# Router logits by linearity: the router's columns ride in the context products of the MLP

## The chip, the cores and the metric

The kernel runs on one core of one Trainium2 chip. The metric is the device time of one execution in microseconds, the median of three runs; lower is better. The engines have queues of their own and meet only at semaphores: TensorE (PE, with its weight loads PEld), VectorE (DVE), ScalarE (ACT), GpSimd (POOL) and SyncE (SP), which issues most of the transfers.

## The reference

`x` is 2 x 1024 tokens of 256 values. Four layers follow one another, each added to `x`: cross attention, attention with four chosen heads, an MLP whose weights are the context itself, and a mixture of eight experts with one expert per token. The change touches the last two.

```python
# third layer: w1 = w2 = ctx_1024[b], 77 x 256
def _L1_xattn_ref(x, w1, w2):              # x here is layernorm(x)
    h = jnp.einsum('eth,efh->etf', x, w1)  # 77 hidden values per token
    g = jax.nn.gelu(h, approximate=True)
    out = jnp.einsum('etf,efh->eth', g, w2)

# fourth layer, x here is layernorm of the new x
    logits = jnp.einsum('bsh,he->bse', x, w_router)
    probs = jax.nn.softmax(logits, axis=-1)
    sel = jnp.argmax(probs, axis=-1)
    wgt = probs at sel
    for e in range(n_experts):
        h = jax.nn.relu(xt @ w1[e] + b1[e])
        y = h @ w2[e] + b2[e]
        out = out + ((sel_t == e) * wgt_t)[:, None] * y
```

## The kernel before

The program is a row of blocks, one after the other: every engine must reach the end of a block before any enters the next. Here the blocks `context_mlp` (it ends at line 1208) and `experts` matter. Everything ahead of them, 390 us, is left as it is.

`context_mlp` works on the 2048 tokens in 16 tiles of 128, in four chunks n = 0 to 3 of four tiles. The order on each engine is written out by hand.

- PE first finishes the attention before it: `attended(r)`, r = 0 to 7, two tiles each. DVE adds the result to `x_all` (`attended` of DVE), takes mean and variance (`statistics`, BN_STATS and BN_AGGR), POOL takes the root, DVE writes the normalised chunk (`normalise`).
- A chunk then goes through `transpose` (PE, 8 transposes into `c_psX`), `copy_x` (ACT, to SBUF), `hidden` (PE, the products with the context, `c_psH`), `square` (ACT), `scaled` (DVE), `tanh` (ACT), `gelu` (DVE, into `c_inner`), `output` (PE, `c_psO`), `update` (DVE, adds to `x_all`), `spread` (DVE, the statistics of the new rows) and `power` (POOL, root and shift). SP stores the finished chunk to the buffer `rows` in DRAM.
- For the router each chunk is sent through PE again, after its `update`: `transpose("route", n)` of `x_all`, a `copy_x`, and `route(n)`, 32 products for all chunks of 128 x 128 weights and 8 columns, into `c_psR`. The list `order` (line 1267) sets how these steps alternate with those of the MLP.
- When all four are there, DVE finds the best expert of every token (lines 1466 to 1472, it writes `c_oh`), PE counts the tokens ahead (`counts`, L1620 and L1622), DVE makes slots of them (L1479 to L1497), PE inverts the list (L1629), DVE writes `src` (L1507), and POOL gathers the rows of the first three groups (L1934). Beside it DVE and PE make the share of each token (L1500 to L1523 and L1633).

The weights of an expert come through a staging buffer `wst` with two places and are split in two parts: ACT rounds (`high_first` for the first matrix, `high_second` for the second), POOL takes the rest of the first (`low_first`), DVE that of the second (`low_second`). The semaphores `high1`, `low1`, `high2`, `low2` count these halves. In the block before, experts 0 and 1 have both halves of their first matrix split, and expert 0 the second matrix rounded.

`experts` runs over tiles of 128 tokens of one expert. PE does `hidden` of tile g (12 products of 512 columns), `transpose_x` of tile g+1, `output` of tile g-1 (24 products), `transpose_h` of tile g. The loop bounds are read from `table` with `bounds(k)`, k loads (L1672) one after the other on the engine's own sequencer; PE reads three before the first `transpose_x`, two behind it and three behind the second. SP fetches the first matrix of expert e+1 when `low1` has reached 2e, then the bias of e, and, when `low2` has reached 2(e-1), the second matrix of e.

Of the kernel before, what the change touches and what calls it, by code (L numbers as in the profile page):

```python
# [19 lines left out]
P = 128  # L20
# [3 lines left out]
CH = 4  # L24
# [17 lines left out]
UNIT = 1.5 * 2 ** 23  # L42
ENDS, TILES, LAST = 2 * TG, 2 * TG + NE - 1, 2 * TG + NE
# [1161 lines left out]
def context_mlp(nc, top, t, io):  # L1205


    with ExitStack() as ctx:
# [7 lines left out]
        ctxT, ctxs, wr = sb("c_ctxT", [P, B, KD, L]), sb("c_ctx", [L, B, D]), t["wr"]  # L1216
# [10 lines left out]
        later = sb("c_inner", [P, 2, CW])  # L1227
        inner = later[0:L]
        spare = later[:].rearrange("p a q -> p (a q)")
        e, first, rank = (spare[:, i * T * NE:(i + 1) * T * NE].rearrange("p (t e) -> p t e", e=NE) for i in range(3))  # L1230
# [10 lines left out]
        passed = spare[:, 3 * T * NE:3 * T * NE + T * TG].rearrange("p (t g) -> p t g", g=TG)  # L1241
# [5 lines left out]
        done_e = spare[0:1, 3 * T * NE + T * TG:3 * T * NE + (T + NE) * TG].rearrange("p (g e) -> p g e", e=NE)  # L1247
# [11 lines left out]
        shares_in = psR_bank[:, T * NE:T * NE + 2 * TG].rearrange("p (x g) -> p x g", x=2)  # L1259
        column = psC[:, 384:384 + NE]  # L1260
        full_ones, wrc = sb("c_full_ones", [P, P]), sb("c_wrc", [P, KD, NE])
# [6 lines left out]
        order = [("mlp", 0), ("mlp", 1), ("mlp", 2), ("route", 0), ("mlp", 3), ("route", 1), ("route", 2), ("route", 3)]  # L1268
# [3 lines left out]
        def _(sp):  # L1272
            sp.dma_start(ctxT[:], io["ctxT"]).then_inc(ctx_in, 16)
# [13 lines left out]
        def _(pool):  # L1287
            link = Link(pool, pool_sem)
            pool.memset(mhalf[:], -0.5)
            pool.memset(full_ones[:], 1.0).then_inc(consts, 1)  # L1290
# [27 lines left out]
            low_first(pool, t, 1, 0)  # L1318
            power(2)
            low_first(pool, t, 1, 1)  # L1320
# [7 lines left out]
        def _(act):  # L1328
            def copy_x(kind, n):
                i = order.index((kind, n))  # L1330
                act.wait_ge(xT_ps, i + 1)
                if i >= 2:
                    user, m = order[i - 2]
                    act.wait_ge(h_ps if user == "mlp" else r_ps, m + 1)
                act.copy(xnT[:, i % 2], psX[:]).then_inc(xT_sb, 1)
# [715 lines left out]
```

## Time and profile before

| | |
|---|---|
| median of 3 runs | 622.28 us (621.88 to 623.95) |
| the profiled execution | 622.69 us |
| its span, first to last instruction | 620.9 us |
| mean granted clock of TensorE in it | 0.943 of full |
| PE busy | 558.7 us, 90% |
| DVE busy | 450.6 us, 73% |
| ACT busy | 356.1 us, 57% |
| POOL busy | 263.6 us, 42% |

A busy share is a mean over stages with different limits. In the rows below a line of the timeline has the start in us from the span's start, the duration, the engine, the line of the kernel, the operation with `out<-in` and its count, and in brackets how long the engine had been idle before and what released it. `PEclk` is the clock that TensorE was granted, as a part of its full 2.4 GHz; 0.50 is 1.2 GHz, and a value between is a stretch in which it changed. A product of 32-bit floats is two passes in the timeline, so four products of `output` show as x8.

### The profile page before, as it was taken

How to read it: one execution, taken by the hardware profiler on the slowest of the kernel's cores; microseconds unless marked ns; L12 is line 12 of the kernel's file. 1: busy time of each engine (PE TensorE's matmuls, PEld its weight loads, DVE VectorE, ACT ScalarE, POOL GpSimd, SP SyncE). 2: the span in 40 equal slices, each digit the busy share in tenths (PEclk: the TensorE clock that was granted, in tenths of full speed). 3: DMA queues.
4: the chain of work that ended last, by engine and by line, in shares of the span. 5: the costliest groups of instructions: out<-in, count | busy, mean ns of one | idle time of the engine just before them, and what ended most of it. 6: DMA issues, size and time to landing. Idle time of an engine off the chain costs nothing. (4 is left out here: it accounts for less than half of the span.)

```text
span 620.9 us, 11787 instructions
## 1 busy us (share of the span) xinstructions
PE 558.7 (90%) x3619; PEld 495.4 (80%) x3620; DVE 450.6 (73%) x909; ACT 356.1 (57%) x727; POOL 263.6 (42%) x288
## 2 busy tenths in 40 slices
PE   4789999994899999999999998899648999999993
PEld 3679999983688888888888887766647899899992
DVE  4888888974138888889888987496664775785672
ACT  3468888753258887788777886035303642662351
POOL 4145545751024443444445343115426572683311
PEclk9879999997899999999999999897658999999998
DMA  8245422200522233222232200722415581671100
GB/s 255 60 119 153 128 52 51 52 1 1 129 51 52 52 73 81 53 51 52 57 84 65 53 1 0 278 99 69 137 30 221 217 287 35 215 250 44 38 26 0
DMA packets 25402, 57.00 MB, mean 92 GB/s; under 512 B 5112, under 2 KB 9977, under 8 KB 23304
## 3 DMA queue, kind: packets, MB, share of 16 engines
q1 hardware_dynamic: 21608, 48.80, 26.9%
q0 software_dynamic: 2256, 5.55, 3.0%
q10 hardware_dynamic: 1488, 2.05, 1.1%
q8 instruction: 24, 0.39, 0.3%
q14 instruction: 26, 0.21, 0.1%
HBM read 33.28 MB, written 4.87 MB: 61 GB/s over the span
## 5 line engine op out<-in xcount | busy, mean ns | idle before, releaser
L987 POOL TENSOR_SCALAR h_p<-h_p,h_rs 128x1024 f32<-128x1024 f32 x64 | 72.5, 1133 | 116.1 <-DVE h_rs L1082 116.0
L1089 DVE TENSOR_REDUCE h_nmx<-h_psS 128x1 f32<-128x1024 f32 x64 | 78.1, 1221 | 28.5 <-PE h_psS L1168 27.1
L1011 ACT CAST h_pTh<-h_psT 128x512 fp32r<-128x512 f32 x128 | 69.2, 590 | 31.3 <-PE h_psT L1126 31.1
L1069 DVE TENSOR_TENSOR h_pTl<-h_psT,h_pTh 128x512 fp32r<-128x512 f32 x128 | 81.4, 677 | 4.5 <-ACT h_pTh L1011 4.5
L1038 ACT ACTIVATE h_p<-h_psS,h_nmx 128x1024 f32<-128x1024 f32 x64 | 72.3, 1129 | 14.0 <-DVE h_nmx L1089 14.0
L1137 PE MATMUL h_psO<-h_pTh,h_vs 128*128 128x256 f32 x256 | 69.9, 306 | 3.0 <-DVE oT L1077 2.2
L1126 PE MATMUL h_psT<-ident,h_p 128*128 128x128 f32 x512 | 67.5, 273 | 1.4 <-DVE h_pTl L1069 1.2
L1126 PEld LDWEIGHTS h_psT<-ident,h_p 128*128 128x128 f32 x512 | 59.3, 141 | 11.4 <-issue 3.3
L1137 PE MATMUL h_psO<-h_pTl,h_vs 128*128 128x256 f32 x256 | 63.6, 282 | 0.0
L380 POOL TENSOR_TENSOR a_p<-a_p,a_rs 128x616 f32<-128x616 f32 x32 | 38.9, 1218 | 53.1 <-DVE a_rs L486 53.1
L1168 PE MATMUL h_psS<-h_kh,h_qs 128*128 128x512 f32 x128 | 55.7, 435 | 0.0
L1137 PEld LDWEIGHTS h_psO<-h_pTh,h_vs 128*128 128x128 f32 x256 | 48.4, 189 | 7.1 <-issue 5.4
L1775 ACT ACTIVATE e_hh<-e_psT 128x512 fp32r<-128x512 f32 x42 | 22.9, 596 | 48.4 <-PE e_psT L1860 44.8
L1168 PE MATMUL h_psS<-h_kl,h_qs 128*128 128x512 f32 x128 | 50.7, 396 | 0.0
L1867 PE MATMUL e_psY<-w2h,e_hh 128*128 (+1 forms) x168 | 48.7, 290 | 1.7 <-DVE e_hl L1826 1.7
L1137 PEld LDWEIGHTS h_psO<-h_pTl,h_vs 128*128 128x128 f32 x256 | 48.6, 190 | 0.3
L1734 POOL DMA_INDIRECT out<-xg,dst x21 | 22.8, 1084 | 60.4 <-DVE xg L1795 59.6
L1867 PE MATMUL e_psY<-w2l,e_hh 128*128 (+1 forms) x168 | 47.0, 280 | 0.0
L1867 PE MATMUL e_psY<-w2h,e_hl 128*128 (+1 forms) x168 | 46.9, 279 | 0.0
L1915 POOL TENSOR_TENSOR w1l<-wst,w1h 128x1024 fp32r<-128x1024 f32 x16 | 38.8, 2441 | 6.6 <-ACT w1h L1909 6.5
L1934 POOL DMA_INDIRECT xg<-rows,src x26 | 27.2, 1046 | 29.5 <-DVE src L1507 14.9
L665 PE MATMUL a_psQ<-a_pT,a_vblk 124*128 124x128 f32 x320 | 38.4, 275 | 0.0
(318 smaller groups left out, 1406.6 us busy)
## 6 DMA issues: line engine op xcount, KB each, us to landing
wst<-in_m_w SPq DMA_DIRECT2D x16, 1024.0 KB, 5.0
bias<-in_m_b SPq DMA_DIRECT2D x8, 640.0 KB, 7.9
h_kh<-h_hi SPq DMA_DIRECT2D x30, 128.0 KB, 2.3
h_kl<-h_lo SPq DMA_DIRECT2D x30, 128.0 KB, 2.4
fw<-in_f_w SPq DMA_DIRECT2D x8, 384.0 KB, 4.0
rows<-x_all SPq DMA_DIRECT2D x4, 518.0 KB, 3.6
a_qs<-a_qhi SPq DMA_DIRECT2D x16, 128.0 KB, 2.3
a_qf<-a_qhi SPq DMA_DIRECT2D x16, 128.0 KB, 2.4
```

The source lines that it names most:

```text
L380: pool.tensor_tensor(p3, p3, rs[:, u, :].unsqueeze(2).to_broadcast([P, HH, L]), ALU.mult).then_inc(pn_ready, 1)
L665: ins = pe.matmul(psQ[:, m, b * P:(b + 1) * P], vblk[:, b, m, c, :], pT[:, n % 2, m, c, b * P:(b + 1) * P], start=(c == 0), stop=(c == VC ...
L987: pool.tensor_scalar(pr[:, u % 4], pr[:, u % 4], rs[:, u:u + 1], 0.0, ALU.mult, ALU.add).then_inc(pn_ready, 1)
L1011: act.copy(pTh[u // QP % 2][:, hf * HK:(hf + 1) * HK, u % QP * P:(u % QP + 1) * P], psT[hf][:]).then_inc(pT_hi, 1)
L1038: act.activation(pr[:, u % 4], psS[u % 2][:], ACT.Exp, bias=nmx[:, u:u + 1], scale=1.0, accum_out=sm[:, u:u + 1]).then_inc(exp_done, 1)
L1069: vec.tensor_tensor(pTl[u // QP % 2][part], psT[hf][:], pTh[u // QP % 2][part], ALU.subtract).then_inc(pT_lo, 1)
L1089: vec.tensor_reduce(nmx[:, u:u + 1], psS[u % 2][:], AX.X, ALU.max, negate=True).then_inc(max_ready, 1)
L1126: ins = pe.transpose(psT[hf][:, k], pr[:, u % 4, (hf * HK + k) * P:(hf * HK + k + 1) * P], ident[:])
L1137: ins = pe.matmul(psO[:, 0:QP * P], vs[i % 2][:, k], part[g % 2][:, k], start=(k == 0 and part is pTh), stop=(k == KT - 1 and part is pTl))
L1168: ins = pe.matmul(psS[u % 2][:, hf * CW:(hf + 1) * CW], qs[i % 2][:, q * P:(q + 1) * P], part[i % 2][:, hf * CW:(hf + 1) * CW], start=(par ...
L1867: ins = pe.matmul(psY[:, 0:D], h_[:, k], w_[:].rearrange("p a w -> p (a w)")[:, bass.ds(at + k * D, D)], start=(k == 0 and n == 0), stop=( ...
L1915: pool.tensor_tensor(halves(t[f"w1l{e % 3}"][:])[:, :, hf], halves(t["wst"][:, e % 2, 0:KD * FF])[:, :, hf], halves(t[f"w1h{e % 3}"][:])[: ...
```

## The change

Three things are changed.

1. **The logits.** The new x is old x plus half of the MLP's output, and logits are linear in x. The weights of `hidden` get 27 more columns: `c_both` holds the 77 context columns, 19 zeros, and at 96 to 103 the router's weights (centred). So `hidden` gives 104 rows instead of 77, the last 8 being the router's products of the normalised old x. ACT copies them beside the gelu into `c_inner`. A matrix `mix` (104 x 16 for each batch) holds the context times the router, computed once by PE (`mix_in`, four products of 8 columns) and scaled by DVE, beside an identity. `route_update(n)`, four products of 16 columns, then gives both parts of the logits of a chunk. DVE puts them together with two operations (`logit`), the old part multiplied by the standard deviation `std`. The second `transpose`, `copy_x` and `route` of each chunk go. `update(3)` and `spread(3)` of DVE move behind the choice of the expert, the constants (lines 1457 to 1462) ahead of `gelu(3)`, and the factor of the exponent behind the lines that make `here`.
2. **The roundings of expert 1.** `high_second` of expert 1 moves from the expert stage into the context stage on ACT; `low_first` of expert 1 moves from the context stage on POOL to behind the gathers 4 and 5 of the expert stage.
3. **The loop bounds.** PE reads two bounds instead of three before the first `transpose_x`, one behind it, and five behind the second.

The core of the diff:

```diff
-        ctxT, ctxs, wr = sb("c_ctxT", [P, B, KD, L]), sb("c_ctx", [L, B, D]), t["wr"]
+        both, ctxs, wr = sb("c_both", [P, B, KD, RW]), sb("c_ctx", [L, B, D]), t["wr"]
+        ctxT = both[:, :, :, 0:L]
...
-            sp.dma_start(ctxT[:], io["ctxT"]).then_inc(ctx_in, 16)
+            for b in range(B):
+                sp.dma_start(ctxT[:, b], io["ctxT"][:, b]).then_inc(ctx_in, 16)
...
             low_first(pool, t, 0, 1)
-            low_first(pool, t, 1, 0)
             power(2)
-            low_first(pool, t, 1, 1)
             power(3)
...
+                if n >= 2:
+                    act.wait_ge(r_ps, n - 1)
+                act.copy(inner[RA:RW, n % 2], psH[n % 2][RA:RW])
...
-            copy_x("route", 1)
-            high_first(act, t, 1, 0)
-            copy_x("route", 2)
-            high_first(act, t, 1, 1)
-            copy_x("route", 3)
-            high_second(act, t, 0, 0)
-            high_second(act, t, 0, 1)
+            for hf in range(2):
+                high_first(act, t, 1, hf)
+            for e_ in range(2):
+                for x in range(2):
+                    high_second(act, t, e_, x)
...
+            vec.wait_ge(count_ps, 2)
+            vec.tensor_scalar(mix[0:L, :, 0], mix_in, 0.5, None, ALU.mult).then_inc(oh_ready, 1)
             normalise(0)
...
+            link(vec.tensor_tensor(logit[:], psR[:], std[:].unsqueeze(2).to_broadcast(full), ALU.mult))
+            link(vec.tensor_tensor(logit[:], psM[:], logit[:], ALU.add))
...
+            vec.wait_ge(rstd_ready, 2 * NC)
+            vec.tensor_tensor(e[:], e[:], rstd4.unsqueeze(2).to_broadcast(full), ALU.mult).then_inc(shifted, 1)
             vec.wait_ge(exp_done, 1)
...
-            def route(n):
+            def route_update(n):
+                pe.wait_ge(g_ready, n + 1)
...
                 for j in range(CH):
-                    for k in range(KD):
-                        ins = pe.matmul(psR[:, n * CH + j], xnT[:, i % 2, k, j * P:(j + 1) * P], wrc[:, k],
-                                        start=(k == 0), stop=(k == KD - 1))
+                    ins = pe.matmul(products[:, n * CH + j], inner[:, n % 2, j * P:(j + 1) * P], mix[:, n // (NC // B)],
+                                    start=True, stop=True)
...
+            pe.wait_ge(ctx_in, 48)
+            for b in range(B):
+                for k in range(KD):
+                    ins = pe.matmul(mix_in[:, b], ctxT[:, b, k, :], wrc[:, b, k], start=(k == 0), stop=(k == KD - 1))
+            ins.then_inc(count_ps, 1)
+            transpose(0)
...
                 gather(pool, t, g)
+                if 4 <= g < 6:
+                    low_first(pool, t, 1, g - 4)
...
                 if e == 0:
-                    bounds(3)
+                    bounds(2)
                     transpose_x(0)
-                    bounds(2)
+                    bounds(1)
...
+                if bounds:
+                    bounds(2)
                 pe.wait_ge(low2, 2 * (e + 1))
                 transpose_h(g)
```

How it moves the instructions, at the three places that the prediction speaks of. First, PE between `attended(4)` and the first `hidden`. Before:

```order
L1535 MATMUL c_psC<-wo,oT 128x256 x4
L1535 MATMUL c_psR<-wo,oT 128x256 x4
L1551 MATMUL c_psX<-ident,xg 128x128 x8
L1535 MATMUL c_psC<-wo,oT 128x256 x4
L1562 MATMUL c_psH<-xg,c_ctxT 77x512 x2
```

And now, with `mix_in` written to `c_psO`:

```order
L1544 MATMUL c_psC<-wo,oT 128x256 x4
L1544 MATMUL c_psR<-wo,oT 128x256 x4
L1597 MATMUL c_psO<-c_both 77x8 x4
L1555 MATMUL c_psX<-ident,xg 128x128 x8
L1544 MATMUL c_psC<-wo,oT 128x256 x4
L1563 MATMUL c_psH<-xg,c_both 104x512 x2
```

The row with `c_psO<-c_both` is new. It stands ahead of the transposes, and DVE waits for it before `normalise(0)`.

Second, PE from `hidden(2)` on, in whose rows `c_psX` are transposes, `c_psH` is `hidden`, `c_psO` `output` and `c_psR` the router's products. Before:

```order
L1562 MATMUL c_psH<-xg,c_ctxT 77x512 x2
L1551 MATMUL c_psX<-ident,x_all 128x128 x8
L1571 MATMUL c_psO<-c_ctx,c_inner 128x256 x4
L1582 MATMUL c_psR<-c_wrc,xg 128x8 x8
L1551 MATMUL c_psX<-ident,xg 128x128 x8
L1562 MATMUL c_psH<-xg,c_ctxT 77x512 x2
L1551 MATMUL c_psX<-ident,x_all 128x128 x8
L1571 MATMUL c_psO<-c_ctx,c_inner 128x256 x4
L1582 MATMUL c_psR<-c_wrc,xg 128x8 x8
L1551 MATMUL c_psX<-ident,x_all 128x128 x8
L1571 MATMUL c_psO<-c_ctx,c_inner 128x256 x4
L1582 MATMUL c_psR<-c_wrc,xg 128x8 x8
```

And now, to the last `output`:

```order
L1563 MATMUL c_psH<-xg,c_both 104x512 x2
L1581 MATMUL c_psR<-c_mix,c_inner 128x16 x4
L1572 MATMUL c_psO<-c_ctx,c_inner 128x256 x4
L1555 MATMUL c_psX<-ident,xg 128x128 x8
L1563 MATMUL c_psH<-xg,c_both 104x512 x2
L1581 MATMUL c_psR<-c_mix,c_inner 128x16 x4
L1572 MATMUL c_psO<-c_ctx,c_inner 128x256 x4
L1581 MATMUL c_psR<-c_mix,c_inner 128x16 x4
L1572 MATMUL c_psO<-c_ctx,c_inner 128x256 x4
```

The three blocks of `x_all` transposes and the three of `c_wrc` products are gone (one more of each followed them); the short rows with `c_mix` stand right behind a `hidden` or an `output`.

Third, DVE around the choice of the expert, where the row that writes `c_oh` starts the counting on PE and the row that writes `c_fits` waits for it. Before:

```order
L1466 TENSOR_REDUCE c_best<-c_psR 128x16
L1468 TENSOR_TENSOR c_inner<-c_psR,c_best 128x128
L1469 SCALAR_TENSOR_TENSOR c_inner<-c_inner,c_num 128x128
L1471 TENSOR_REDUCE c_low<-c_inner 128x16
L1472 TENSOR_TENSOR c_oh<-c_inner,c_low 128x128
L1474 TENSOR_TENSOR c_inner<-c_psR,c_best 128x128
L1476 TENSOR_TENSOR c_inner<-c_inner,x_all 128x128
L1479 TENSOR_TENSOR c_fits<-c_psC,c_steps 128x128
```

And now (one product of `c_psR` with `c_std` stands ahead of the first row):

```order
L1472 TENSOR_TENSOR xg<-c_psR,xg 128x128
L1473 TENSOR_REDUCE c_best<-xg 128x16
L1475 TENSOR_TENSOR xg<-xg,c_best 128x128
L1476 SCALAR_TENSOR_TENSOR xg<-xg,c_num 128x128
L1478 TENSOR_REDUCE c_low<-xg 128x16
L1479 TENSOR_TENSOR c_oh<-xg,c_low 128x128
L1410 SCALAR_TENSOR_TENSOR x_all<-c_psO,x_all 128x4x256
L72 BN_STATS c_stats<-x_all 128x6 x4
L75 BN_AGGR x_all<-c_stats 128x2 x4
L1416 TENSOR_SCALAR x_all<-x_all 128x4
L1483 TENSOR_TENSOR xg<-xg,c_best 128x128
L1486 TENSOR_TENSOR c_fits<-c_psC,c_steps 128x128
```

Between `c_oh` and `c_fits` there are now `update(3)` (L1410) and `spread(3)` (BN_STATS, BN_AGGR, L1416). The second exponent operation is gone from here.

## Rows read from the trace of the kernel before

**Rows 1.** Stretches of 2 us: busy PE, PEld, DVE, ACT, POOL; clock; DMA, GB/s.

```profile
422.00:424.00 2.00, 2.00 (x18) 2.00 (x18) 1.97 (x5) 0.00 (x0) 1.53 (x4) 0.91 0.00 0
...
426.00:428.00 2.00, 2.00 (x3) 0.80 (x4) 0.22 (x1) 0.87 (x1) 1.72 (x5) 0.50 0.20 67
...
430.00:432.00 2.00, 2.00 (x13) 1.87 (x12) 0.68 (x1) 1.25 (x3) 0.19 (x1) 0.88 0.19 64
...
440.00:442.00 2.00, 1.04 (x5) 1.04 (x6) 1.17 (x11) 2.00 (x3) 1.71 (x3) 0.68 0.39 128
...
470.00:472.00 2.00, 2.00 (x7) 1.58 (x6) 0.69 (x1) 0.00 (x0) 0.00 (x0) 0.64 1.04 399
```

**Rows 2.** Timeline of DVE in the context stage.

```profile
401.27 1.37 DVE L1381 TENSOR_SCALAR xg<-x_all,mv,rstd 128x256 f32<-128x256 f32 x4
...
430.34 0.68 DVE L1400 SCALAR_TENSOR_TENSOR c_inner<-c_sq,c_psH 77x512 f32<-77x512 f32 x1 [4.12 <-ACT c_sq L1339]
432.77 1.23 DVE L1410 SCALAR_TENSOR_TENSOR x_all<-c_psO,x_all 128x1024 f32<-128x1024 f32 x1 [1.74 <-PE c_psO L1571]
...
437.28 1.23 DVE L1410 SCALAR_TENSOR_TENSOR x_all<-c_psO,x_all 128x1024 f32<-128x1024 f32 x1 [0.76 <-PE c_psO L1571]
...
440.47 0.17 DVE L1457 CAST c_tok<-c_toki 128x16 f32<-128x16 int32 x1
...
441.32 0.06 DVE L1462 MEMSET c_steps<- 128x1 f32 x1
444.58 0.29 DVE L1466 TENSOR_REDUCE c_best<-c_psR 128x16 f32<-128x128 f32 x1 [3.20 <-PE c_psR L1582]
...
445.88 0.29 DVE L1472 TENSOR_TENSOR c_oh<-c_inner,c_low 128x128 bf16<-128x128 f32 x1
...
447.55 0.29 DVE L1479 TENSOR_TENSOR c_fits<-c_psC,c_steps 128x128 f32<-128x128 f32 x1 [0.85 <-PE c_psC L1622]
...
455.95 0.19 DVE L1507 TENSOR_SCALAR src<-c_psC 128x26 int32<-128x26 f32 x1 [0.41 <-PE c_psC L1629]
```

**Rows 3.** Timeline of PE in the context stage.

```profile
400.61 1.99 PE L1535 MATMUL c_psR<-wo,oT 128*128 128x256 f32 x8
...
416.99 1.94 PE L1562 MATMUL c_psH<-xg,c_ctxT 128*77 128x512 f32 x4 [1.10 <-ACT xg L1335]
418.77 1.04 PE L1551 MATMUL c_psX<-ident,x_all 128*128 128x128 f32 x8
...
421.46 1.95 PE L1582 MATMUL c_psR<-c_wrc,xg 128*128 128x8 f32 x16
...
425.98 3.70 PE L1562 MATMUL c_psH<-xg,c_ctxT 128*77 128x512 f32 x4 [1.10 <-ACT xg L1335]
...
440.96 3.58 PE L1582 MATMUL c_psR<-c_wrc,xg 128*128 128x8 f32 x16 [1.10 <-ACT xg L1335]
```

**Rows 4.** Timeline of ACT in the context stage.

```profile
431.06 0.63 ACT L1343 ACTIVATE c_sq<-c_inner 77x512 f32<-77x512 f32 x1 [0.75 <-DVE c_inner L1400]
```

**Rows 5.** Line 1208, the end of the context block: duration ns, start us.

```profile
L1208 POOLq DRAIN  x1: 5887/5887/5887, 457.9 to 457.9; - x1
```

**Rows 6.** Line 1672, loads on PE's sequencer from 464 to 466 us.

```profile
L1672 PEldq TENSOR_LOAD <-table x3: 308/313/492, 464.2 to 465.7; - x3
```

**Rows 7.** Timeline of PE at the first expert tile.

```profile
466.36 0.68 PE L1842 MATMUL e_psX<-ident,oT 128*128 128x128 f32 x2 [6.05 <-issue]
468.05 0.77 PE L1851 MATMUL e_psH<-w1h,e_xh 128*128 128x512 f32 x1 [1.01 <-DVE e_xl L1786]
```

**Rows 8.** Timeline of POOL, gathers around the start of the expert stage.

```profile
460.20 1.00 POOL L1934 DMA_INDIRECT xg<-rows,src  x1 [0.31 <-issue]
...
472.83 1.00 POOL L1934 DMA_INDIRECT xg<-rows,src  x1 [4.00 <-DMA xg<-rows,src]
```

**Rows 9.** Timeline of ACT, rounding of the second matrix of expert 2.

```profile
495.28 2.00 ACT L1922 CAST w2h<-wst 128x1024 fp32r<-128x1024 f32 x2
```

**Rows 10.** Timeline of SyncE's queue, the fetch of that matrix.

```profile
466.51 0.33 SPq L1958 DMA_DIRECT2D wst<-in_m_w  x1
```

More of the change, by code:

```diff
@@ L1226, in context_mlp @@
         sq = sb("c_sq", [L, 2, CW])
[L1227 to L1230, printed above, removed]
+        inner = sb("c_inner", [RW, 2, CW])
+        spare = flat[:, 2 * (2 * CH * D):]
+        e, first, rank, logit = (spare[:, i * T * NE:(i + 1) * T * NE].rearrange("p (t e) -> p t e", e=NE) for i in range(4))
         oh = sb("c_oh", [P, T + 1, NE], BF16)
@@ L1289, in _ @@
             pool.memset(mhalf[:], -0.5)
+            pool.memset(both[:, :, :, L:RA], 0.0)
             pool.memset(full_ones[:], 1.0).then_inc(consts, 1)
@@ L1448, in _ @@
             spread(1)
+            vec.scalar_tensor_tensor(std[:], mv[:, :, 1], EPS, rstd[:], ALU.add, ALU.mult)
             scaled(3)
-            update(2)
-            gelu(3)
-            spread(2)
-            update(3)
-            spread(3)
             vec.wait_ge(consts, 2)
@@ L1461, in _ @@
             link(vec.memset(steps[:, :, 0:1], -1.0))
-            vec.memset(steps[:, 0, 1:2], -1.0)
+            link(vec.memset(steps[:, 0, 1:2], -1.0))
+            gelu(3)
+            update(2)
+            spread(2)
             vec.wait_ge(r_ps, NC)
             full = [P, T, NE]
-            link(vec.tensor_reduce(best[:], psR[:], AX.X, ALU.max))
+            link(vec.tensor_tensor(logit[:], psR[:], std[:].unsqueeze(2).to_broadcast(full), ALU.mult))
+            link(vec.tensor_tensor(logit[:], psM[:], logit[:], ALU.add))
+            link(vec.tensor_reduce(best[:], logit[:], AX.X, ALU.max))
             most = best[:].unsqueeze(2).to_broadcast(full)
-            link(vec.tensor_tensor(first[:], psR[:], most, ALU.is_equal))
+            link(vec.tensor_tensor(first[:], logit[:], most, ALU.is_equal))
             link(vec.scalar_tensor_tensor(first[:], first[:], -float(NE), num[:, 0:NE].unsqueeze(1)
@@ L1473, in _ @@
                               ALU.is_equal).then_inc(oh_ready, 1)
-            link(vec.tensor_tensor(e[:], psR[:], most, ALU.subtract))
-            vec.wait_ge(rstd_ready, 2 * NC)
-            vec.tensor_tensor(e[:], e[:], rstd4.unsqueeze(2).to_broadcast(full), ALU.mult).then_inc(shifted, 1)
-            vec.wait_ge(count_ps, 2)
+            update(3)
+            spread(3)
+            vec.tensor_tensor(e[:], logit[:], most, ALU.subtract)
+            vec.wait_ge(count_ps, 3)
             link(vec.tensor_tensor(fits[:], counts[:, T].unsqueeze(2).to_broadcast([P, NE, T]),
@@ L1759, in change @@
                     return
-                for x in range(2):
-                    high_second(act, t, e, x)
+                if e >= 2:
+                    for x in range(2):
+                        high_second(act, t, e, x)
                 if e + 2 < NE:
```

114 lines of the change are left out of this document (52 added, 62 removed).

## The prediction

> **What bounds the kernel now.** I looked at the page first for the stage that the change touches: the context block, 391 to 464 us, then at the stretches of 2 us for which engine is full, then at the timelines of PE and DVE, and last at the end of the block. The reader is to see a chain that changes its engine. Up to about 426 us DVE is full and PE nearly: `hidden(2)` on PE waits 1.10 us for ACT's copy and DVE has 1.97 of 2 us busy at 422 [rows 1, 3]. From 426 to 444.5 it is PE: DVE is busy 0.22 of 2 us and waits 4.12 us before `scaled(3)` and 3.20 us before the choice of the expert, each time for a result that comes from PE [rows 1, 2]. What PE does there is the rest of the MLP and the second transposes, copies and `route` steps, partly at the low clock of 1.2 GHz: it was granted 0.91 of full at 422 to 424, 0.50 at 426 to 428, 0.88 at 430 to 432 [rows 1]. From 444.58 on DVE and PE alternate to `src` at 455.95, then POOL gathers until 461.2 and its drain ends at 463.8, which opens the expert stage [rows 2, 5, 8]. There the first tile waits for PE's loads of bounds, and from 468.05 on PE is the bound to the end.
>
> **The change, step by step along this chain.** All positions are in the time of the profiled execution before.
>
> a) The wait for `mix_in`. DVE is ready for `normalise(0)` at 401.27 [rows 2]; PE's `attended(4)` ends at 402.60, and `mix_in` comes behind it: 8 passes. A `route` step has 16 passes in 1.95 us [rows 3]; 0.15 of it overlaps the next block, so 0.11 each, 0.9, and 0.1 for the end. With the scaling on DVE (0.2, between nothing and the 0.29 of a wider operation [rows 2]) `normalise(0)` starts near 403.75: +2.45. Behind this wait stand all of DVE's steps, and PE's transposes wait for them, so nothing absorbs it. The 27 more columns of `hidden` are the other operand of the array and should not lengthen it (the rows are the same for 77 of them; if they do, by 27/77 of its four passes, it is +0.7 each, my bound). The new memsets lie in DVE's and POOL's wait for the first PE products; they cost at most 0.15, which is in the 2.45.
>
> b) `route_update(0)` stands ahead of `output(0)`: 8 passes again, +0.9. `hidden(2)` would start at 420.4 instead of 416.99. ACT's new copy of 8 rows lies in its wait for `scaled`, 0.75 us before the `tanh` [rows 4]; its cost is between nothing and the 0.63 of an operation of the same width. Without that cover it would be 0.6 for each of four chunks.
>
> c) From `hidden(2)` to `hidden(3)` there are 8.99 us. Out go the transposes of `x_all` (1.04 less the overlap, 0.87 [rows 3]) and `route(0)` (1.8), and some 0.7 of the low clock and of gaps; in comes `route_update(1)` (0.9): -2.5.
>
> d) `hidden(3)` takes 3.70 at the low clock, `hidden(2)` 1.94 at the full one [rows 3]. The clock fell at 423.6 (0.91 over 2 us is 0.36 us at half [rows 1]), just behind `route(0)`, a block of 16 passes with 8 columns each. This block is gone and nothing like it, only half as long, is left: -1.8.
>
> e) From the end of `hidden(3)` (429.68) to the end of `c_oh` (446.17) there are 16.5 us. In the new kernel DVE has this to do: wait for the `square`, 0.65; `scaled(3)` 0.6; the constants, 440.47 to 441.38, 0.95, beside which ACT does the `tanh`; `gelu(3)`, `update(2)` and `spread(2)`, 432.77 to 436.52, 3.75; two new operations for the logits, 0.33 each, 0.65; and the choice, 444.58 to 446.17, 1.6 [rows 2, 4]. That is 8.2: -8.3. PE's `route_update(3)` and `output(3)` lie beside it. ACT is free for the four roundings that it gets there.
>
> f) Behind `c_oh` DVE had 1.38 us until the counts were there (447.55). Now `update(3)` and `spread(3)` come in between, 437.28 to 440.47, 3.2: +1.8. `power(3)` and the store of the last chunk follow, by my estimate 6 us of the nearly 10 until the gathers need them.
>
> g) The exponent waits now: about 0.3 for the factor on DVE and 0.3 on ACT, with 0.1 for the two signals. DVE had 0.41 idle before `src` [rows 2]: +0.3. The drain of POOL and the gathers keep their length.
>
> h) Expert stage: PE's three loads run from 464.2, 0.7 to 0.8 apart, and the transposes start at 466.36, put down to issue [rows 6, 7]. One load less is -0.7; what follows them, ACT's copy and DVE's `x_low`, for which PE waits 1.01 us [rows 7], comes earlier with them, unless DVE's `low_second`, which is ahead of `x_low`, is then the later one: it costs 0.2 to 0.5 of the 0.7 at most, my bound. The two loads that move behind the second transposes run while the array still works through the first `hidden`.
>
> i) The clock at the experts: it rose at 471.4 (0.64 over 2 us is 1.44 us at half), 3.4 us after the first product at 468.05; after `hidden(3)` began at 425.98 it took 4.5, to 430.5 [rows 1, 3, 7]. The first is the luckier one; 1.1 us longer at half speed is 0.55, I take +0.4.
>
> j) Expert 1's halves. `low_first` on POOL, two operations of some 2.4, now stand between the gathers 4 and 6. POOL had waited 4.00 us there for a gather to land [rows 8], since SP's fetches filled the queue, and these fetches now wait for the same `low1`. They come some 8 us later than at 466.51; the last of them is needed by ACT at 495.28 [rows 9, 10]. 29 us less 8, and some 7 for moving 2.7 MB, leaves 14: zero. ACT's two roundings that leave the expert stage were not waited for.
>
> The sum: 2.45 + 0.9 - 2.5 - 1.8 - 8.3 + 1.8 + 0.3 - 0.7 + 0.4 = -7.45 us. The profiled execution took 622.69 (span 620.9 and 1.8 around it), so 615.2; it lies 0.4 above the median of 622.28, so the median to expect is **614.8 us**.
>
> A rule that speaks against step d: the Trainium skill, "TensorE: Matmul & The Clock Gate", Part 4, says that transposes don't count as work for the clock in the way products do. By this the stretch of `route_update`, transposes and the wait for ACT before `hidden(3)` would look empty, and the clock would fall there as before. What this trace shows is that `hidden(2)`, after transposes and a wait of 1.10 us, took 1.94 us and so ran at the full clock [rows 3]. It speaks against the rule, but the same two steps with a short product block ahead are not in the trace. By the rule the time would be 616.6, by the row 614.8.
>
> **The rivals.**
>
> B, the clock falls once more before `hidden(3)`. For it: in both falls of this block, near 423.6 and 440.7, PE had done a router step and transposes and then waited 1.10 us [rows 1, 3], and a shorter form of that remains. Against it: the `route` steps were twice as long. Step d is then nothing: 614.8 + 1.8 = 616.6.
>
> C, the short products are slower than I price them. If their passes cost what those of `attended` do, 8 in 1.99 less the end, 0.22 each [rows 3], the three on the path (`mix_in` and two `route_update`) cost 0.9 more each: 617.5. For it: they load weights of 104 or 128 rows for 16 columns, a shape that the trace lacks; against it the `route` steps, the nearest row. In the other direction, if two of them vanish behind waits, it is 613.0.
>
> D, on the other side: the PE steps taken out are hidden anyway, because DVE's own queue is the bound to the end of the block. Then c, d and e give nothing, the waits added stay (2.45 + 0.9 + 1.8 + 0.3 - 0.7 + 0.4 = +5.2), and it is 627.4. It decides itself at `scaled(3)`: if DVE comes there later than ACT's `square`, the PE work did not matter. Against it: DVE waits 4.12 us at this place and 3.20 us before the choice [rows 2]; the added 3.4 us must outweigh both, and they move PE and DVE alike.
>
> E, the expert stage starves, because all fetches hang on POOL's two moved operations: for any loss the fetch at 466.51 must come 22 us later instead of 8. To lose the 7.45, it must come 29 later: 622.3 and more. Against it are the 14 us of room in j.
>
> **How the numbers follow.** The forecast, from 613.3 to 616.0, has 0.62; B 0.16; C 0.10 (of it 0.03 below); D 0.04; E 0.03; the 0.05 left are for a gain that is smaller by something not seen, of which 0.02 is inside 0.3% of no change. The range, 612.9 to 617.8, takes in B and C. A change of under 0.3%, 1.9 us, can't be told from none here. Faster: 0.62 + 0.16 + 0.10 + 0.03 = 0.91; same 0.03 with a part of E; slower 0.06.
>
> **What would show it.** In the profile after: `normalise(0)` near 403.8 and a DVE wait of some 2.3 us before the scaling (a); `hidden(2)` near 420.4 and `hidden(3)` near 426.9 with about 1.9 us (b to d); `c_oh` ending near 437 (e), `c_fits` near 440.1 (f), `src` near 448.8 (g), the drain over near 456.7, the first expert product near 460.2 (h), and no wait of PE in the expert stage after that (j). I am wrong if `hidden(3)` takes over 3 us (B), if a `route_update` takes over 1.5 us (C), if DVE has no wait left before `scaled(3)` and `c_oh` comes after 440 (D), or if PE waits for `w1h` or `w2h` among the experts (E).

## The result and the profile after

| | before | after |
|---|---|---|
| median, 14 runs each | 622.40 us (620.84 to 624.00) | 619.52 us (616.32 to 621.08) |
| ratio, 95% interval | | 0.9943 [0.9926, 0.9959] |
| the profiled execution, its span | 622.69, 620.9 us | 620.80, 619.0 us |
| mean granted clock | 0.943 | 0.943 |

The kernel is 2.9 us faster, not 7.5. To see where the rest is, the profiled execution is cut in four at instructions that both kernels have: the first PE product of the context block, the first product of the experts, and the last PE product.

| us | before | after | difference |
|---|---|---|---|
| everything ahead, to the first product of the context block | 391.35 | 392.69 | +1.34 |
| context block, to the first product of the experts | 76.70 | 68.64 | -8.06 |
| expert stage, to the start of the last product | 143.85 | 148.65 | +4.80 |
| what is left of the measured time | 10.79 | 10.82 | +0.03 |

The context block gained what the forecast said. The expert stage gave over half of it back, and it was forecast at +0.4.

**The context block.** DVE's timeline (columns as in [rows 2]):

```profile
404.48 0.17 DVE L1434 TENSOR_SCALAR c_mix<-c_psO 77x16 f32<-77x16 f32 x1 [1.77 <-PE c_psO L1597]
404.57 1.37 DVE L1381 TENSOR_SCALAR xg<-x_all,mv,rstd 128x256 f32<-128x256 f32 x4
...
430.44 0.67 DVE L1400 SCALAR_TENSOR_TENSOR c_inner<-c_sq,c_psH 77x512 f32<-77x512 f32 x1
...
435.77 0.28 DVE L1471 TENSOR_TENSOR xg<-c_psR,c_std 128x128 f32<-128x128 f32 x1
...
437.73 0.29 DVE L1479 TENSOR_TENSOR c_oh<-xg,c_low 128x128 bf16<-128x128 f32 x1
437.94 1.22 DVE L1410 SCALAR_TENSOR_TENSOR x_all<-c_psO,x_all 128x1024 f32<-128x1024 f32 x1
...
441.12 0.29 DVE L1483 TENSOR_TENSOR xg<-xg,c_best 128x128 f32<-128x128 f32 x1
441.32 0.28 DVE L1486 TENSOR_TENSOR c_fits<-c_psC,c_steps 128x128 f32<-128x128 f32 x1
...
449.90 0.18 DVE L1516 TENSOR_SCALAR src<-c_psC 128x26 int32<-128x26 f32 x1
```

`normalise(0)` now waits for `mix_in` (1.77 us of idle time ahead of the scaling). `scaled(3)` has no idle time ahead of it where it had 4.12, and the choice of the expert none where it had 3.20 [rows 2]: from 426 us on DVE is the engine that is full. `update(3)` (437.94) and the one row of the exponent (441.12) stand between `c_oh` and `c_fits`. PE in the same block, to be held against [rows 3]:

```profile
403.78 0.66 PE L1597 MATMUL c_psO<-c_both 128*77 128x8 f32 x8
405.99 1.09 PE L1555 MATMUL c_psX<-ident,xg 128*128 128x128 f32 x8 [1.55 <-DVE xg L1381]
...
416.41 0.96 PE L1581 MATMUL c_psR<-c_mix,c_inner 104*128 104x16 f32 x8
...
421.17 1.96 PE L1563 MATMUL c_psH<-xg,c_both 128*104 128x512 f32 x4 [1.10 <-ACT xg L1337]
...
427.74 1.96 PE L1563 MATMUL c_psH<-xg,c_both 128*104 128x512 f32 x4 [1.10 <-ACT xg L1337]
429.54 0.96 PE L1581 MATMUL c_psR<-c_mix,c_inner 104*128 104x16 f32 x8
```

The 8 passes of `mix_in` took 0.66 us, a `route_update` 0.96, and `hidden` is no longer with 104 columns than with 77 (1.96 against 1.94). `hidden(3)` took 1.96 where it had taken 3.70. In stretches of 2 us (columns as in [rows 1]):

```profile
422.00:424.00 2.00, 2.00 (x12) 1.38 (x11) 1.07 (x4) 0.80 (x2) 0.00 (x0) 1.00 0.00 0
426.00:428.00 2.00, 0.90 (x7) 0.65 (x6) 1.97 (x7) 1.33 (x2) 1.33 (x3) 1.00 0.00 0
434.00:436.00 2.00, 2.00 (x8) 1.35 (x8) 1.93 (x10) 2.00 (x3) 0.57 (x2) 0.87 0.34 115
464.00:466.00 2.00, 2.00 (x6) 1.58 (x5) 0.69 (x1) 0.00 (x0) 1.91 (x2) 0.50 0.13 29
466.00:468.00 2.00, 1.87 (x13) 1.44 (x13) 1.05 (x2) 0.43 (x2) 1.84 (x2) 0.95 0.10 37
496.00:498.00 2.00, 1.89 (x10) 1.60 (x11) 1.83 (x6) 0.90 (x2) 1.66 (x3) 0.73 0.91 381
498.00:500.00 2.00, 2.00 (x6) 1.54 (x5) 1.17 (x2) 0.78 (x2) 2.00 (x1) 0.50 0.98 397
500.00:502.00 2.00, 2.00 (x11) 1.68 (x10) 0.95 (x2) 0.00 (x0) 2.00 (x2) 0.91 1.03 361
```

Before, the clock was 0.91 at 422 and 0.50 at 426 [rows 1]; both stretches are now at full clock. The second fall is still there, at 435.5, and lasts until 466.2. A third one is new: 0.73, 0.50 and 0.91 between 496 and 502, in the middle of the expert stage.

**The expert stage.** What stands ahead of that fall, on PE, DVE, POOL, and then SyncE's queue:

```profile
459.64 0.68 PE L1846 MATMUL e_psX<-ident,oT 128*128 128x128 f32 x2 [5.40 <-ACT oT L1747]
461.33 0.77 PE L1855 MATMUL e_psH<-w1h,e_xh 128*128 128x512 f32 x1 [1.01 <-DVE e_xl L1790]
...
496.11 1.55 PE L1864 MATMUL e_psT<-ident,oT 128*128 128x128 f32 x8 [2.08 <-DVE oT L1821]
```

```profile
483.06 2.39 DVE L1934 TENSOR_TENSOR w2l<-wst,w2h 128x1024 fp32r<-128x1024 f32 x2
...
490.38 5.08 DVE L1934 TENSOR_TENSOR w2l<-wst,w2h 128x1024 fp32r<-128x1024 f32 x2 [0.52 <-ACT w2h L1928]
495.38 1.27 DVE L1821 TENSOR_TENSOR oT<-e_psH,bias 128x512 f32<-128x512 f32 x2
```

```profile
461.51 2.39 POOL L1921 TENSOR_TENSOR w1l<-wst,w1h 128x1024 fp32r<-128x1024 f32 x1
...
465.11 2.38 POOL L1921 TENSOR_TENSOR w1l<-wst,w1h 128x1024 fp32r<-128x1024 f32 x1
...
475.40 1.02 POOL L1940 DMA_INDIRECT xg<-rows,src  x1 [0.67 <-issue]
482.86 1.03 POOL L1737 DMA_INDIRECT out<-xg,dst  x1 [6.45 <-DVE xg L1799]
...
488.62 5.75 POOL L1921 TENSOR_TENSOR w1l<-wst,w1h 128x1024 fp32r<-128x1024 f32 x2 [0.28 <-issue]
```

```profile
467.51 0.34 SPq L1954 DMA_DIRECT2D wst<-in_m_w  x1
467.90 0.44 SPq L1959 DMA_DIRECT2D bias<-in_m_b  x1
468.37 0.43 SPq L1964 DMA_DIRECT2D wst<-in_m_w  x1
```

Read from the bottom: SP issues the fetches of expert 3 and of expert 2's second matrix together at 467.5 to 468.4, behind the two `low_first` at 461.51 and 465.11; before, they went at 464.08 and 466.51 (the first row of the block below, and [rows 10]), that is 4.0 and 1.5 us ahead of the first expert product instead of 6.2 and 7.0 behind it. POOL's first output row comes at 482.86, behind 6.45 us of idle time, though the result that the trace names as its releaser was there from 475.3 on. All that POOL does next is late with it, so that its `w1l` of expert 3 (488.62) runs beside DVE's `w2l` of expert 2 (490.38), which takes 5.08 us instead of the 2.39 at 483.06. Behind `w2l` in DVE's queue stands the bias addition (`oT`, 495.38) that PE's transposes need: PE waits 2.08 us at 496.11, and right behind it the clock is low for 3.4 us. In the kernel before PE has no wait there. Its rows for the first of these fetches, DVE's `w2l` of expert 2 and POOL's `w1l` of expert 3:

```profile
464.08 0.35 SPq L1948 DMA_DIRECT2D wst<-in_m_w  x1
...
496.36 2.50 DVE L1928 TENSOR_TENSOR w2l<-wst,w2h 128x1024 fp32r<-128x1024 f32 x2 [0.39 <-ACT w2h L1922]
...
491.59 5.05 POOL L1915 TENSOR_TENSOR w1l<-wst,w1h 128x1024 fp32r<-128x1024 f32 x2 [1.01 <-ACT w1h L1909]
```

Counted from the first expert product, POOL's pair started at 23.5 us and was nearly over when DVE's `w2l` came at 28.3. Now it starts at 27.3, and DVE's comes at 29.1.

The 4.80 us of the expert stage can be added up: 2.08 for PE's wait, 1.70 for the new fall of the clock (3.4 us at half speed), 0.75 for the later rise of the clock at the start of the stage; 0.3 is left.

### The profile page after: what moved, and what is told of

The parts are those of the page before. It is cut to its first block and busy times, and to the rows that moved or that the text cites. A ratio compares the mean times of both kernels' runs of the same rounds, so it can differ in the third digit from the quotient of the medians.

```text
span 619.0 us, 11677 instructions
## 1 busy us (share of the span) xinstructions
PE 551.3 (89%) x3564; PEld 488.8 (79%) x3564; DVE 454.7 (73%) x917; ACT 354.7 (57%) x727; POOL 264.5 (43%) x289
## 5 line engine op out<-in xcount | busy, mean ns | idle before, releaser
L1821 DVE TENSOR_TENSOR oT<-e_psH,bias 128x512 f32<-128x512 f32 x42 | 28.1, 684 | 15.0 <-PE e_psH L1855 12.7
```

## The experiments

They are three series, e1 to e4, e5 to e8 and e9 to e11, each on a chip of its own. A ratio is against the kernel before in the same series, so that runs of two series are compared by their ratios rather than by their medians. The stages are those of the table above, from one profiled execution each. By their ratios e1 and e3 to e11 are faster than before, e2 slower, each by 1.4% or less, with intervals that exclude no change.

| run | median, us | ratio, 95% interval | context | experts |
|---|---|---|---|---|
| e1 both roundings back | 619.17 | 0.9925 [0.9900, 0.9949] | 71.74 | 144.78 |
| e2 roundings alone | 625.26 | 1.0033 [1.0007, 1.0058] | 76.71 | 145.81 |
| e3 POOL's rounding back | 619.62 | 0.9934 [0.9913, 0.9956] | 73.24 | 143.71 |
| e4 ACT's rounding back | 619.56 | 0.9954 [0.9925, 0.9982] | 68.77 | 148.31 |
| e5 the changed kernel again | 618.79 | 0.9938 [0.9913, 0.9964] | 68.78 | 146.52 |
| e6 `w1l` waits for `w2l` | 618.90 | 0.9934 [0.9909, 0.9959] | 68.78 | 146.09 |
| e7 scaling of `mix_in` late | 616.83 | 0.9898 [0.9861, 0.9935] | 65.22 | 146.84 |
| e8 POOL's rounding early | 616.21 | 0.9889 [0.9850, 0.9927] | 68.76 | 144.54 |
| e9 e7 and e8 together | 614.78 | 0.9888 [0.9862, 0.9913] | 67.12 | 144.92 |
| e10 e9, fetches late | 613.95 | 0.9868 [0.9840, 0.9896] | 66.98 | 145.81 |
| e11 loads of bounds back | 619.13 | 0.9958 [0.9937, 0.9980] | 69.55 | 146.19 |

e5 shows how far one profile may be trusted: the same code has an expert stage of 146.52 us here and 148.65 above. The wait is there in both (`w2l` took 4.07, PE waited 1.62), the fall of the clock behind it only in the first. For the changed kernel the loss in the expert stage is thus 2.7 to 4.8 us.

**e1, both roundings of expert 1 where they were.**

```diff
             low_first(pool, t, 0, 1)
+            low_first(pool, t, 1, 0)
             power(2)
+            low_first(pool, t, 1, 1)
             power(3)
```

and `high_second(act, t, 1, x)` back in the expert stage; the logits as changed.

> The changed kernel with expert 1's roundings back at their old places (both halves of low_first in the context stage on POOL, high_second at the change to expert 1 on ACT); logits and loop bounds as changed. Theory 1, the moved roundings cost the missing time, since POOL's w1l of expert 3 and DVE's w2l of expert 2 now run together (w2l 5.08 us instead of 2.36, PE waits 2.08, clock falls): 615 to 616.5 us, no PE wait in the expert stage, w2l at most 2.5. Theory 2, the moved roundings don't matter and the time was lost elsewhere (other clock phase, the context stage): 619.5 us as with the whole change.

The expert stage is back at 144.78 and PE's wait is gone, as Theory 1 said, but the context block is 3.1 us longer, and the time isn't the 615 to 616.5 us of that theory: it is the same as with the whole change. DVE and POOL of e1, at the choice of the expert:

```profile
436.61 1.15 DVE L1417 TENSOR_SCALAR x_all<-x_all 128x4 f32<-128x4 f32 x1
...
439.63 2.24 DVE L1480 TENSOR_TENSOR c_oh<-xg,c_low 128x128 bf16<-128x128 f32 x1
```

```profile
433.05 4.68 POOL L1919 TENSOR_TENSOR w1l<-wst,w1h 128x1024 fp32r<-128x1024 f32 x2
...
439.38 2.34 POOL L1919 TENSOR_TENSOR w1l<-wst,w1h 128x1024 fp32r<-128x1024 f32 x1
```

`c_oh`, 0.29 us elsewhere, takes 2.24 and ends at 441.87, beside a `w1l` that ends at 441.72; the 128x4 operation at 436.61 takes 1.15 instead of 0.17 and ends with the other `w1l`. The same two engines that meet among the experts meet here on the path to `src`. The two rows together are 2.9 us longer than elsewhere, which is what `c_oh` ends later than in the changed kernel (48.23 against 45.33 us behind the first product of the block). So the new order needs POOL's rounding out of this place, or loses this.

**e2, the roundings moved in the kernel before, nothing else.** The reverse of e1's edit on the old code.

> The kernel before with nothing but the roundings of expert 1 moved. Theory 1: 3 to 4 us slower than before, 625 to 626.5 us, a w2l of some 5 us beside a w1l of POOL and a PE wait near the start of expert 2. Theory 2: 622.3, as before.

It is 2 us slower than before (the interval goes from 0.4 to 3.6), as expected of the move, and its expert stage is 1.96 longer; POOL's idle time before its first output is 5.69 us, a `w2l` takes 4.30, PE waits 1.31. The move costs by itself, without any change of the logits.

**e3 and e4, the two roundings apart:** e3 has POOL's back and ACT's moved, e4 the other way round.

> The changed kernel with only low_first of expert 1 back on POOL in the context stage; high_second stays early. Theory 1a, what makes POOL late is the move of low_first and the burst of fetches behind it (POOL stood 6.4 us before its first scatter): 615 to 616.5 us. Theory 1b, it is the earlier first-matrix rounding of expert 3 on ACT: 619 us. Theory 2: 619.5.

> The changed kernel with only high_second of expert 1 back at the change of experts; low_first stays behind the gathers. Theory 1a: the clash stays or gets later, 618 to 620 us. Theory 1b: 615 to 616.5. Theory 2: 619.5.

e3 has no wait of PE behind DVE's `oT` in the expert stage, `c_oh` at 2.23 us as in e1, and POOL's first output 0.30 us behind its gather; e4 has the `w2l` of 5.11 us and PE's wait of 2.1 us as the changed kernel has. So it is POOL's part alone. e3's time missed its 615 to 616.5 us for the same reason as e1's, and its profiled execution has a second early fall of the clock besides. ACT's two operations cost nothing that these runs can resolve, as forecast.

**e5 and e6: again, and without the meeting.**

```diff
                                 with pool.If(e == x):
+                                    if x == 1:
+                                        pool.wait_ge(low2, 6)
                                     for hf in range(2):
                                         low_first(pool, t, x + 2, hf)
```

> The changed kernel itself, as a base for the three others on the same chip. 0.994 of before, as measured; w2l of expert 2 near 5 us beside POOL's w1l, a PE wait of about 2 us and a fall of the clock behind it.

> The changed kernel, with POOL made to wait for both halves of w2l of expert 2 before its w1l of expert 3. Theory 1, DVE's two-operand operation from the local memory stands while a POOL operation runs, and this alone holds PE: w2l back to 2.4 us, no PE wait at expert 2, no clock fall, 3.5 to 4 us less than the changed kernel in a run that has the clash, 616 us. Theory 3, w2l is long because the weights or the DMAs come late: w2l stays at 4 to 5 us, 619.5.

In e6 `w2l` takes 2.36 us and PE doesn't wait for it, but the time is that of e5. POOL's `w1l` comes at 491.84, and PE waits elsewhere:

```profile
509.58 0.39 PE L1857 MATMUL e_psH<-w1l,e_xh 128*128 128x512 f32 x1
511.06 0.44 PE L1848 MATMUL e_psX<-ident,oT 128*128 128x128 f32 x2 [1.08 <-issue]
```

So Theory 3 falls: the weights were there, and `w2l` is long because of POOL's operation beside it. Theory 1 is borne out for `w2l` and for PE's wait behind it, not for the time. But the edit does two things. It takes the meeting away by making POOL wait 3.77 us more, so that its `w1l` starts 31.1 us behind the first expert product instead of e5's 26.4. The new wait, of 1.08 us, is in no other trace. Ahead of it ACT's `e_hh` came late (508.46 and 509.92, behind 4.47 and 0.86 us of idle time); what held it isn't shown. e6 thus shows what makes `w2l` long, and not what the kernel would take without the meeting and with POOL on time. That is e8.

**e7, the scaling of `mix_in` behind `scaled(0)`,** so that nothing waits for it.

```diff
-            vec.wait_ge(count_ps, 2)
-            vec.tensor_scalar(mix[0:L, :, 0], mix_in, 0.5, None, ALU.mult).then_inc(oh_ready, 1)
             normalise(0)
...
             scaled(0)
+            vec.wait_ge(count_ps, 2)
+            vec.tensor_scalar(mix[0:L, :, 0], mix_in, 0.5, None, ALU.mult).then_inc(oh_ready, 1)
             statistics(2)
```

> The changed kernel, with DVE's wait for mix_in and its scaling moved from ahead of normalise(0) to ahead of statistics(2), where mix_in is long done. If the wait costs what it shows, 1.8 us plus the gap of PE behind it, and the clock fall that followed this gap in two of the four last profiles: 2 to 3 us less than the changed kernel, 617. If the rest of the chain swallows it: same as the changed kernel.

PE of e7, `mix_in` and the transposes behind it:

```profile
402.64 0.66 PE L1597 MATMUL c_psO<-c_both 128*77 128x8 f32 x8
403.15 1.07 PE L1555 MATMUL c_psX<-ident,xg 128*128 128x128 f32 x8
```

The 1.55 us of idle time ahead of 405.99 in the changed kernel is gone. The trace has 3.4 us less in the context block, but half of that isn't the edit's: in this execution the clock did not fall at 394 us, where it fell in the changed kernel (0.63 and 0.51 at 394 to 398) and in e9. Like for like, from the first product to `c_oh`, it is 43.32 us in e9 against 45.04: 1.7. The medians say 2.0 (616.83 against 618.79), near the 617 expected, with intervals that overlap (0.9861 to 0.9935 against 0.9913 to 0.9964).

**e8, POOL's rounding of expert 1 as early as it goes without meeting `c_oh`:** one half behind the first three gathers, one behind the fourth.

```diff
             for g in range(3):
                 gather(pool, t, g)
+            low_first(pool, t, 1, 0)
...
                 gather(pool, t, g)
-                if 4 <= g < 6:
-                    low_first(pool, t, 1, g - 4)
+                if g == 3:
+                    low_first(pool, t, 1, 1)
```

> The changed kernel, with low_first of expert 1 placed where DVE has nothing to do: its first half behind the three gathers of the context block (beside the drain, 2.65 us), its second right behind gather 3. The fetches then start 5 us earlier. If the burst of fetches is what keeps POOL from its first scatter, this gap of 6.4 us is gone, w1l of expert 3 ends before w2l of expert 2 begins, and it is 616. If the gap stays, 619.5.

The fetches go out at 464.4 to 465.3, only 1.4 to 2.2 us behind the first expert product (changed kernel: 6.2 to 7.0). POOL of e8:

```profile
456.76 2.35 POOL L1922 TENSOR_TENSOR w1l<-wst,w1h 128x1024 fp32r<-128x1024 f32 x1
...
461.92 2.45 POOL L1922 TENSOR_TENSOR w1l<-wst,w1h 128x1024 fp32r<-128x1024 f32 x1
...
477.80 1.01 POOL L1941 DMA_INDIRECT xg<-rows,src  x1 [0.16 <-issue]
479.12 1.03 POOL L1738 DMA_INDIRECT out<-xg,dst  x1 [0.30 <-issue]
```

The first output follows its gather 0.30 us later, every `w2l` takes 2.35 to 2.50, PE doesn't wait, and the kernel is 2.6 us faster than the changed one of the same series, with intervals that just overlap (0.9850 to 0.9927 against 0.9913 to 0.9964). POOL's `w1l` of expert 3 starts 24.4 us behind the first expert product and DVE's `w2l` of expert 2 at 29.0, nearly as before. This is the failed step taken out.

**e9, e7 and e8 together; e10, the same with the fetches late; e11, the loads of bounds undone.** e10 makes SyncE wait for the first tile's `hidden`:

```diff
             for e in range(2, NE):
+                if e == 2:
+                    sp.wait_ge(h_ps, 2)
                 if e + 1 < NE:
```

and in the changed kernel e11 has

```diff
                 if e == 0:
-                    bounds(2)
+                    bounds(3)
                     transpose_x(0)
-                    bounds(1)
+                    bounds(2)
...
                 pe.reg_mov(second_at, e % 2 * FB * D)
-                if bounds:
-                    bounds(2)
```

> The changed kernel with the scaling of `mix_in` behind `scaled(0)` (no wait ahead of `normalise(0)`) and with the two `low_first` of expert 1 behind the first gathers, both together. If the two gains stand in different stages, as the traces of each alone have it, they add: context stage 65.2 us as with the late scaling, expert stage 144.5 as with the early rounding, together 209.7 against 217.3 of the changed kernel's profiled run: a time near 613 us, 0.985 of before. If the start of the expert stage is set by something that doesn't move with the context stage (the fetches of the weights), the gain doesn't add and the time stays near 616, with a wait of PE in the expert stage.

> The kernel of both edits, with one thing more: SyncE waits for the second half of the first tile's `hidden` before it issues the fetches of expert 3 and of the second matrix, so that they start some 5 us after the first expert product, as in the changed kernel, while POOL's roundings stay at their early place. Theory (the late burst of fetches holds POOL up before its first output, and that puts `low_first(3)` beside `low_second(2)`): a gap of 5 us or more between POOL's last gather there and the first output, `w2l` of expert 2 over 4 us on DVE, a wait of PE of 1.5 to 2 us before the third or fourth tile, and an expert stage of 146.5 to 148.5 us, 2 to 4 us longer than with both edits alone. Rival (it was the two roundings between the gathers that made POOL late, not the fetches): the gap is 1.3 us or less, no wait of PE, the same time as with both edits within 1 us.

> The changed kernel with all three loads of bounds ahead of the first transposes again and none behind the second, the rest as changed. Theory: the first transposes of the expert stage start 0.7 us later after the end of the context block, the first product of the experts as much; the time is 0.3 to 0.7 us above the changed kernel's, near its uncertainty. Rival (DVE's `low_second` or ACT's copy is what the first product waits for, or the waits further on take the 0.7 us back): the first product comes within 0.2 us of the changed kernel's and the time is the same.

e9 is 7 us faster than before by its ratio, 8 by the medians. The expert stage is as expected (144.92), the context block 1.9 longer than expected from e7's trace, of which 1.7 is the fall of the clock at 394 that e7's execution lacked. In the stages the two gains add: 1.6 us less than e8 in the context block, no loss among the experts. In the time this isn't shown. e9's ratio, 0.9888, is that of e8 alone (0.9889), and the forecast 0.985 lies just outside its interval, though inside e10's.

e10 tells what delays POOL's first output. That output, first of e9 and then of e10:

```profile
467.35 4.74 POOL L1922 TENSOR_TENSOR w1l<-wst,w1h 128x1024 fp32r<-128x1024 f32 x2 [0.52 <-DMA xg<-rows,src]
472.24 1.01 POOL L1941 DMA_INDIRECT xg<-rows,src  x1
473.67 1.03 POOL L1738 DMA_INDIRECT out<-xg,dst  x1 [0.42 <-issue]
```

```profile
465.13 4.76 POOL L1924 TENSOR_TENSOR w1l<-wst,w1h 128x1024 fp32r<-128x1024 f32 x2
470.04 1.02 POOL L1943 DMA_INDIRECT xg<-rows,src  x1 [0.16 <-issue]
475.59 1.03 POOL L1740 DMA_INDIRECT out<-xg,dst  x1 [4.53 <-issue]
```

POOL's pair of roundings and its last gather are 2.2 us earlier in e10 than in e9, the fetches go out at 463.1 to 464.4 instead of 459.7 to 461.0, and the idle time before the output is 4.53 us instead of 0.42. So it is the time of the fetches, not the two operations in POOL's row, that makes the gap: the rival falls.

What in the fetches holds POOL isn't shown. The trace hints at POOL's own code. In each of the eight traces with a gap of over 4 us, an 8 KB packet of the queue `q14 instruction` comes 1.94 to 2.00 us ahead of the output row, and in the changed kernel and e10 DMA is nearly full until then (share 0.85 to 1.08). In the other five traces the last such packet comes 1.93 to 3.39 us ahead, and POOL isn't held. That the queue is POOL's, and that this packet is what it waits for, is argued, not tested.

The rest of e10 isn't what its theory says. A `w2l` takes 4.55 us again and PE waits 1.48, but it is the `w2l` of expert 1, one earlier than in the changed kernel:

```profile
480.16 4.55 DVE L1937 TENSOR_TENSOR w2l<-wst,w2h 128x1024 fp32r<-128x1024 f32 x2
...
481.15 5.78 POOL L1924 TENSOR_TENSOR w1l<-wst,w1h 128x1024 fp32r<-128x1024 f32 x2
```

POOL's `w1l` isn't late here: it starts 22.5 us behind the first expert product, 24.3 in e9. The gap was made good before POOL's second output, for which e9's POOL waits 3.54 us for DVE's result and e10's 0.80. The meeting comes from the other side. DVE's `w2l` of experts 1 and 2 start 6.7 to 8.6 us apart and take 2.4 each, and POOL's pair takes 4.75, so it barely fits between them. It does where it starts 23.0 to 24.4 us behind the first expert product (before, e1, e3, e8 and e9). In six traces it starts at 25.6 to 27.3 and meets the `w2l` of expert 2, in e10 at 22.5 and meets that of expert 1.

The price was expected at 2 to 4 us, and the expert stage is 0.9 longer than e9's. Of this PE's waits are +1.6 and the clock -1.4, as it rose 3.0 us behind the first expert product instead of 5.8; 0.7 is left. The wait costs about what it shows, and the earlier rise hides it in this execution. e10's time is not above e9's (613.95 against 614.78, intervals that overlap): 1.5 us of PE's waiting is near what these comparisons can resolve.

e11 has its first expert product 0.77 us later in the block than e5, as forecast (0.7), and a time that can't be told from the changed kernel's.

## Why the prediction was wrong

The direction and the context block were right, the size was wrong: 614.8 us was forecast, 619.5 came. Against the profiled execution (forecast 615.2, measured 620.80) 5.6 us are missing: 4.4 in the expert stage, 1.3 ahead of the context block, and -0.2 in it.

Step by step, each between the same instructions of the two profiles:

| step | forecast | measured |
|---|---|---|
| a) to `normalise(0)` | +2.45 | +1.96 |
| b) to `hidden(2)` | +0.9 | +0.88 |
| c) to `hidden(3)` | -2.5 | -2.42 |
| d) `hidden(3)` | -1.8 | -1.74 |
| e) to the end of `c_oh` | -8.3 | -8.17 |
| f) `c_oh` to `c_fits` | +1.8 | +1.92 |
| g) `c_fits` to `src` | +0.3 | +0.18 |
| h) `src` to the first expert product | -0.7 | -0.67 |
| i), j) the expert stage | +0.4 | +4.80 |

- **a)** The wait is as described; the passes of `mix_in` are shorter than the 0.9 that I took, 0.66. DVE's memset takes 0.91 us, not 0.15, but DVE's first addition comes 2.96 us behind the first PE product against 3.22 before, so it is covered. The wait can be avoided (e7).
- **b) to d)** `route_update` takes 0.96, as priced (0.9), so rival C falls. `hidden(3)` stood behind 8 short passes, an `output`, transposes and a wait of 1.10 us, and the clock was full: the combination that the trace of before lacked. Rival B falls with it, and not by the luck of one execution: the clock was full there in all eleven traces with the new logits. One reading behind B was off: the fall near 423.6 came just behind the transposes' start (423.27) and ahead of PE's wait of 1.10 us, not behind it; only the fall near 440.7 came in such a wait. The rule of the Trainium skill ("TensorE: Matmul & The Clock Gate", Part 4) spoke for a fall here; this row is against it, in this case.
- **e) to h)** DVE's row, added up operation by operation, was the right account of e. The sign given for rival D came true in half: DVE has no wait left before `scaled(3)` (430.44), since `spread` and `c_std` keep it there; the 0.65 forecast as a wait for the `square` is its own work. But `c_oh` came at 437.7 and not after 440. The prediction's test, that PE's work did not matter if DVE came there late, was a bad one: DVE is full now because the 4.12 and 3.20 us that it had waited for PE are gone. ACT's copy of 8 rows takes 0.58 us, as much as an operation of 77 rows (0.59), and lies in ACT's idle time. h is borne out by e11.
- **i)** The clock rose at 466.2, 4.9 us after the first expert product instead of 3.4: half of 1.5 is 0.75 for the forecast 0.4. The size was off; in e5 and e8 it was 4.4 and 4.75, in e9 5.8, in e10 3.0.
- **j) is the step that failed:** "29 us less 8, and some 7 for moving 2.7 MB, leaves 14: zero". It asked only whether the weights would arrive in time, and they did: PE waits nowhere for `w1h` or `w2h`, and rival E, as it was told, did not happen. It did not ask what the later fetches lie beside, nor what POOL's other work would then lie beside. They hold POOL up: its idle time before the first output is 6.45 us in the changed kernel, 4.53 in e10 where only the fetches are late, 0.30 in e8 where they are early. POOL's `w1l` moves beside DVE's `w2l` (5.08 us for 2.36), and DVE's row holds PE. That is 1.6 to 2.1 us of waiting of PE in the two traces of this code, 1.7 more where the clock falls behind it, and the move alone measures +2 us in the old kernel (e2). That the meeting follows from the gap is read from the rows of the changed kernel and of e8; e10, meant to show it, met at another place.

The sum over e1 to e5 and e8 is plain: the new logits are worth the forecast's 8 us only if POOL's rounding leaves the place beside `c_oh`; put among the gathers it costs the experts 2.7 to 4.8; put right behind the first gathers (e8) 0.7, which the later rise of the clock (4.75 us instead of 3.4, at half speed) accounts for.

The 1.3 us ahead of the block are not the change's: its first instruction on POOL comes 0.76 us behind the start of DVE's last row of the block before in both profiles, and what precedes is untouched code; 0.1 us lies between it and the first product and may be the change's. Over the runs with the changed logits the block's first product lies anywhere from 391.19 to 394.29. It is a limit of forecasting from one execution: with e5's profile the time would have been missed by 3.1 instead of 5.6.

## What to carry to other kernels

When operations move from one stage to another, cost them where they land: write down what the other engine of the pair DVE and POOL does at the new time, and everything that waits on the same semaphore, SP's fetches above all. A transfer with 14 us of room can still do harm, by what its burst lies beside. And an edit that takes a wait away by putting another in (e6) tells what made the wait, not what it costs: for the cost, move the work to where it meets nothing (e8).

## What the runs showed of the hardware

DVE's operations with both inputs in SBUF wait while a `tensor_tensor` of POOL runs: `w2l`, 2.36 us elsewhere, took 3.98 to 5.11 in seven traces, `c_oh` 2.24 instead of 0.29 (e1). An in-place `tensor_scalar` of 128x4 took 1.15 instead of 0.17 and ended with POOL's operation (e1). Operations with an input in PSUM took their usual time beside it: two `e_hl` at 488.58 of the changed kernel 1.28 us, beside the `w1l` at 488.62.

The Trainium skill, "SBUF — State Buffer", section "Who interferes with whom", says the same: with two SBUF inputs such an operation contends with a POOL instruction that reads SBUF, and the one that starts first holds the other off. The runs agree. Where DVE came first, POOL paid: its pair took 5.03 us instead of 4.75 (e9), as it did in the kernel before (5.05 at 491.59). In a longer meeting the two can take turns, one instruction each: in the changed kernel DVE's first `w2l` ended 1.1 us behind POOL's first `w1l`, POOL's second then took 3.38 instead of 2.4, and DVE's second 3.42 instead of 1.2. In e4 and e5 POOL ran both of its operations before DVE's first could end.

The clock of PE has falls that come and go between executions of one code: near 394 us in all traces here but those of e1, e7 and e11; at 404 to 407, near the wait for `mix_in`, in e1, e3 and e11 and in no other, at 497 behind PE's wait in the changed kernel and in e4, not in e5. Each is 3.4 us at half speed, which is 1.7 us of PE's time and more than half of what the whole change brings.
